# Layer 0 of a graph network: one-hots of the matmul lots compared on VectorE instead of turned on TensorE, with the helper steps of the next batch in other places

## What is computed

```
h = relu(layernorm(x))
for each head:
    feat = h @ W[head];  alpha_s = feat @ a1;  alpha_d = feat @ a2
    logit = leaky_relu(alpha_s[src] + alpha_d[dst], 0.2)
    e = exp(logit - segment_max(logit, src)[src])
    att = e / segment_sum(e, src)[src]
    out = relu(segment_sum(att * feat[dst], src))
x = x + concat(out)
```

## Time and profile before

| | us |
|---|---|
| median of 3 runs | 3007.26 (3004.64 to 3008.09) |
| span of the profiled execution | 3541.0 |
| PE busy | 2699.5 |
| DVE busy | 2161.8 |
| POOL busy | 1858.0 |
| ACT busy | 995.2 |

### The profile page before, as it was taken

The page is one execution under the profiler, slowest core; times in us unless marked ns, Lnnn a source line. Parts: engine busy times, 40 slices in busy tenths (PEclk is TensorE's granted clock), DMA queues, the critical chain, the costliest instruction groups (busy, mean ns, idle before and its releaser), DMA issues. The chain is left out here.

```text
span 3541.0 us, 46052 instructions
## 1 busy us (share of the span) xinstructions
PE 2699.5 (76%) x10647; PEld 1671.1 (47%) x10692; DVE 2161.8 (61%) x3783; ACT 995.2 (28%) x3078; POOL 1858.0 (52%) x1883
## 2 busy tenths in 40 slices
PE   6887377777777877777777787877778788788991
PEld 4554256666656656655656652323333333233440
DVE  9999966666666767666668743333333333334668
ACT  6733334444443444434444520000000000000220
POOL 0000255555555556555555446666666666664667
PEclk8998678898988899898898897888889999999995
DMA  5110366666666666666665856666666666565226
GB/s 184 47 40 31 111 180 185 186 189 185 180 182 188 180 191 189 183 192 176 177 189 191 288 152 174 176 180 178 178 176 178 173 173 175 171 174 157 67 66 251
DMA packets 243449, 588.25 MB, mean 166 GB/s; under 512 B 57744, under 2 KB 82832, under 8 KB 243400
## 3 DMA queue, kind: packets, MB, share of 16 engines
q0 software_dynamic: 133120, 443.52, 43.8%
q1 hardware_dynamic: 110280, 144.14, 12.4%
HBM read 533.43 MB, written 54.10 MB: 166 GB/s over the span
## 5 line engine op out<-in xcount | busy, mean ns | idle before, releaser
L506 POOL DMA_INDIRECT big<-feat_table,idx x880 | 841.3, 956 | 1020.8 <-ACT idx L531 407.5
L1133 POOL DMA_INDIRECT big<-h_table,idx x784 | 743.6, 948 | 460.6 <-issue 235.2
L801 PE MATMUL psA<-big,onehot 128*128 128x260 f32 x1760 | 504.0, 436 | 120.1 <-DVE big L683 95.4
L801 PE MATMUL psB<-big,onehot 128*128 128x260 f32 x1760 | 479.8, 420 | 18.6 <-DVE acc L693 13.1
L801 PEld LDWEIGHTS psA<-big,onehot 128*128 128x128 f32 x1760 | 365.4, 216 | 208.3 <-issue 115.2
L557 ACT ACTIVATE big<-big,late_weights 128x65 f32<-128x65 f32 x1760 | 434.4, 343 | 0.0
L801 PEld LDWEIGHTS psB<-big,onehot 128*128 128x128 f32 x1760 | 351.5, 209 | 84.9 <-DVE acc L693 22.2
L531 ACT CAST idx<-minorB 128x8 int32 (+1 forms) x101 | 20.4, 204 | 1142.6 <-DMA big<-h_table,idx 1142.6
L1565 DVE TENSOR_TENSOR acc<-acc,psCD 128x512 f32 x176 | 120.7, 686 | 320.1 <-remote 106.2
L1565 DVE TENSOR_TENSOR acc<-acc,psA 128x512 f32 x176 | 120.7, 686 | 273.6 <-remote 103.3
L1859 PE MATMUL psA<-big,onehot 128*128 x352 | 199.3, 650 | 58.9 <-issue 42.7
(11 more groups left out here) (447 smaller groups left out, 3960.8 us busy)
## 6 DMA issues: line engine op xcount, KB each, us to landing
nodes_all<-slot_nodes SPq DMA_DIRECT2D x56, 512.0 KB
big<-feat_table,idx POOLq DMA_INDIRECT x880
feat_table<-big SPq DMA_DIRECT2D x49, 264.0 KB, 2.1
x_table<-acc SPq DMA_DIRECT2D x49, 256.0 KB, 3.8
h_table<-big SPq DMA_DIRECT2D x49, 256.0 KB, 4.0
big<-h_table,idx POOLq DMA_INDIRECT x784
big<-h_table SPq DMA_DIRECT2D x49, 256.0 KB, 2.6
big<-x_table SPq DMA_DIRECT2D x49, 256.0 KB, 4.3
```

The source lines that it names most:

```text
L506: g.indirect_dma_start(ring[:, b.k, q * SB + u, :], None, feat_table, bass.IndirectOffsetOnAxis(ap=idx[:, 2 * b.k + q, u:u + 1], axis=0)). ...
L801: ins = pet.matmul(psum[:, 512 * hf:512 * hf + HALF_W], onehot[:, q, u % SB, :], ring[:, b.k, u, HALF_W * hf:HALF_W * (hf + 1)], start=(u ...
L1133: g.indirect_dma_start(big[:, place:place + D], None, h1_table, bass.IndirectOffsetOnAxis(ap=idx[:, r.c % CHUNK_CYCLE, b:b + 1], axis=0)). ...
```

## The change

The float32 one-hots are no longer turned by PE and cast by ACT. The sorted source nodes, turned once in the setup, are kept in a tile `nodeA` (bfloat16). In each slot DVE, behind `add_lot`, compares the one-hots of the same lot of `nxt`: 128 node numbers in PSUM against the nodes of two chunks, 256 elements on each partition. PE's lots wait for them one by one. `turn_logits` stands one lot sooner on PE, `sum_ends` too; `local_runs` stands in slot 3 of DVE in place of 4, `carry_runs` in 5 in place of 4, `find_tops` and `make_factors` in 6 in place of 5. The second look-up stands behind lot 7. `pad_keys`, `nodeA` and `maxd` share one tile `spare`.

```diff
+        spare = sb("spare", [P, PAD_SPAN + TILES * H], F32)
+        nodeA = spare[:, 0:COLS // 2].bitcast(BF16).rearrange("p (b r) -> p b r", b=SB)
-        onehot_ps = psC[:, 0:512].bitcast(BF16)
+        numbers0 = psC[:, 0:P]
@@ layer0_sync
+            sp.wait_ge(look_ps, 2 * (BATCHES + 1))
@@ layer0_scalar
-            def keep_onehot(b, q):
-                act.wait_ge(turned_ps, b(2, q + 1))
-                s.copy(onehot[:, q, :, :].rearrange("p b n -> p (b n)"), onehot_ps).then_inc(onehot_ready, 1)
                 s.copy(logit, logit_ps).then_inc(logit_kept, 1)
-                keep_onehot(b, 0)
...
                 keep_parts(b.ahead(1))
-                if this:
-                    act.wait_ge(lot_ps, this(LB, LB + RING_CREDIT))
-                keep_onehot(b, 1)
...
+            act.wait_ge(fieldsT, 2)
+            act.wait_ge(nodes_out, 1)
+            s.copy(nodeA.rearrange("p b r -> p (b r)"), psB[:, :]).then_inc(nodes_kept, 1)
             clear_rest()
@@ layer0_vector
-                wait_count(dve, turned_ps, b(2, q - 1))
+                wait_count(dve, look_ps, b(2, q - 1))
...
+            def make_onehot0(b, a):
+                q, u = a // LOTS, 2 * a % SB
+                dve.wait_ge(lot_ps, b(LB, a + 1 - LB + RING_CREDIT))
+                v.tensor_tensor(onehot[:, q, u:u + 2, :], numbers0.unsqueeze(1).broadcast_to([P, 2, P]),
+                                nodeA[:, u:u + 2, bass.ds(b(2, q), 1)].broadcast_to([P, 2, P]), ALU.is_equal).then_inc(onehot_ready, 1)
...
-                        if a == 4:
+                        if a == 3:
                             local_runs(nxt)
+                        if a == 5:
                             carry_runs(nxt)
-                        if a == 5:
                             make_onehotT(aft, 1)
+                        if a == 6:
                             find_tops(nxt)
                             make_factors(nxt)
...
                         add_lot(this, a, tiles[a % LOTS])
...
-                    if nxt and a == 1:
-                        make_onehotT(aft, 0)
+                    if nxt:
+                        make_onehot0(nxt, a)
+                        if a == 1:
+                            make_onehotT(aft, 0)
...
+            link(v.tensor_copy(numbers0, iota_row[:, :]))
@@ layer0_tensor
-            def turn_onehot(b, q):
-                wait_count(pe, onehot_ready, b(2, q))
-                for u in range(SB):
-                    ins = pet.transpose(onehot_ps[:, u * P:(u + 1) * P], onehotT[q][:, u * P:(u + 1) * P], ident_b)
-                ins.then_inc(turned_ps, 1)
...
-                if a % LOTS == 0:
-                    pe.wait_ge(onehot_ready, b(2, q + 1))
+                pe.wait_ge(onehot_ready, b(LB, a + 1))
...
-                    if a == 0:
-                        turn_onehot(nxt, 0)
+                    if a == 2:
+                        turn_logits(nxt)
                     if a == 3:
-                        turn_logits(nxt)
-                    if a == 4:
                         sum_ends(nxt)
-                        turn_onehot(nxt, 1)
                     if a == 5:
                         spread_carries(nxt)
                     if a == 6:
-                        for q in range(2):
-                            look_up(aft, q, tiles[q])
+                        look_up(aft, 0, tiles[0])
                         spread_factors(nxt)
                         turn_weights(nxt)
+                    if a == 7:
+                        look_up(aft, 1, tiles[1])
```

More of the change, by code:

```diff
@@ L139, in build @@
         iota_pad = sb("iota_pad", [P, PAD_COLS], F32)
-        pad_keys = sb("pad_keys", [P, PAD_SPAN], I32)
+        spare = sb("spare", [P, PAD_SPAN + TILES * H], F32)
+        pad_keys = spare[:, 0:PAD_SPAN].bitcast(I32)
+        nodeA = spare[:, 0:COLS // 2].bitcast(BF16).rearrange("p (b r) -> p b r", b=SB)
         ones = sb("ones", [P, H], F32)
@@ L151, in build @@
         alphas = sb("alphas", [P, TILES, 2 * H], F32)
-        maxd = sb("maxd", [P, TILES, H], F32)
+        maxd = spare[:, PAD_SPAN:].rearrange("p (t h) -> p t h", t=TILES)
         Wa = sb("Wa", [P, KD, 2 * H], F32)
@@ L333, in build @@
         rows_arrived = [sem(f"rows_arrived{n}") for n in range(2 * ARRIVAL_GROUPS)]
-        turned_ps = sem("turned_ps")
+        nodes_kept = sem("nodes_kept")
         onehot_ready = sem("onehot_ready")
@@ L721, in pass_batch @@
                             tiles = load_tiles(dve, tileA, this(2, 1))
-                    if nxt and a == 1:
-                        make_onehotT(aft, 0)
+                    if nxt:
+                        make_onehot0(nxt, a)
+                        if a == 1:
+                            make_onehotT(aft, 0)
             dve.wait_ge(acc_zeroed, 3)
             dve.sem_inc(lot_added, ADD_CREDIT)
+            link(v.tensor_copy(numbers0, iota_row[:, :]))
+            dve.wait_ge(nodes_kept, 1)
             link(v.memset(running[0:H, 1, CH:CH + 1], -BIG))
```

## The result

| | median of the runs, us | range, us |
|---|---|---|
| before | 3007.65 | 3004.64 to 3008.09 |
| after | 3177.98 | 3174.15 to 3179.82 |

The ratio is 1.0572, with a 95% interval of 1.0559 to 1.0585: slower by 170 us. The forecast was 3110 with 2960 to 3195 around it; the sign and the range held, and the median lies 68 us above the forecast.

A forecast was written before the change was run, and what follows sets the result against it. POOL's gathers were taken to bound both loops, at 20.05 us a pass in layer 0. The new pass was 17.8 + 2.6 + 1.5 = 21.9 us; 54 x 1.85 = 100, plus 2, gave about 3110 us, range 2960 to 3195.

The forecast's parts named there:

- clock falls behind the end sums: PE's lot 4 in layer 0's loop: slowdown after idling, left out of the sum and priced only as rival B.
- rival B: PE idles some 3 us before the end sums, clock falls, lot 4 late by 1.9 us: 103 on top, 3213 us; chance 0.14.
- DVE waits for lot 4: Layer 0's loop: lot 4 queues on PE behind the end sums, so DVE waits 1.48 us in each pass.
- DVE's work over the gathers' pace: Layer 0's loop: comparisons raise DVE's work from 17.8 to 20.4 us a pass, passing POOL's 20.05.
- What bounds the kernel: Both layers' loops run at POOL's gather pace without a profile, 20.05 us a pass in layer 0; nameless waits come from recording.
- Rival A: Gathers faster than 1.25 us without a profile, so DVE's 19.1 us chain binds today: 3160 us; chance 0.10.
- C: PE's stalls partly real, and the new order relieves DVE's waits in layer 0: faster, 2945 us; chance 0.20.
- D: Landing of the gathers sets the pass at about 21.9 us, comparisons fill DVE's waits: 3007 us; chance 0.10.
- The cost of a comparison: Each 256-element DVE comparison takes about 420 ns, adding 0.33 us a step, 2.6 us a pass (ends 2.2 and 4.9).
- DVE's slack: Layer 0's loop before: DVE's chain of 19.1 us a pass leaves 0.95 us under the gathers' pace.
- The waits at the old L635 and L652: DVE's waits for `sum_ends` (0.4 us a pass) and `spread_carries` (0.9) go in the new order.

The follow-up runs named there:

- filler: Changed kernel plus 12 float32 matmuls on PE just ahead of the end sums, product overwritten by lot 4: 3116.58 us, ratio 1.0378.
- end sums later: Changed kernel with the end sums back behind lot 4 on PE, all else as changed: 3035.55 us, ratio 1.0112.
- fewer gathers: Kernel before with 12 of 16 gathers issued in a pass from batch 2 on (results wrong): 2984.43 us, ratio 0.9937.
- the two and eight operations: Kernel before plus two or eight unused 256-element DVE operations a pass: 3012.74 us (ratio 1.0035) and 3086.2 us (ratio 1.0288).
- the order alone: Kernel before's one-hots (PE turns, ACT casts) with the change's slots for the other steps: 3025.45 us, ratio 1.0077.
- Comparisons alone: Changed kernel's one-hot comparisons with every step of the order back in its slot of before: 3067.6 us, ratio 1.0218.

## Why the prediction was right in sign and 68 us short

The 172 us (1.0572 x 3003) divide as follows, each part from two runs that differ in it (the filler itself costs some 5 us, which stand in the second part and are missing from the first):

| part | from | us | forecast |
|---|---|---|---|
| clock falls behind the end sums | after less filler | 58 | 0 (rival B: 103) |
| DVE waits for lot 4 | filler less end sums later | 80 | 1.48 x 54 = 80 |
| DVE's work over the gathers' pace | end sums later less before | 34 | 0.35 x 54 = 19 |

**What bounds the kernel.** Right. Both loops ran at the pace of their gathers (20.04 us a pass against 20.05), and the nameless waits were the recording's. In layer 0 the run with fewer gathers tests this; in layer 1 only the match of the times and POOL's row speak for it. Rival A, faster gathers and no slack, fell with the same two runs and with the two and eight operations. (A slip in the working: eight lots at 1.81 us are 14.5 us, not 14.1; nothing hangs on it.) C, which had PE's stalls partly real, fell with that, and so did the gain it promised. D fell too: the pass follows DVE's load.

**The cost of a comparison.** Right in what one takes, 416 ns for about 420. What it adds to DVE's busy time is a bit less than forecast: 1093.96 us with the end sums one lot later, less 976.27 before, is 117.7 over 432 comparisons, 0.27 us each and 2.2 us a pass. That is the low end of the range given, and 2.6 was taken.

**DVE's slack.** Mis-sized: 0.95 forecast, 0.4 measured (fewer gathers). The forecast counted two waits of DVE's chain and missed two of 0.33 us a pass. Here two errors nearly cancel: with the end sums later, DVE's busy time is 19.9 us a pass, not 20.4, and its pass is 20.64, since some 0.7 us of small gaps remain that the forecast put at nothing.

**The new wait of DVE for lot 4.** Right in place, mechanism and size: 1.48 us forecast, 1.47 with the clock kept up. PE waits at L778 in every pass, DVE behind it, and the wait is gone when the end sums stand behind the lot. The waits at the old L635 and L652 went as forecast. The pass without the clock's part would be 21.9 us by the forecast and is 22.1.

**The clock.** This is the step that failed, and most of the 68 us: it was put at nothing in the sum and measured 58. The forecast worked out PE's idle time before the end sums well (some 3 us; 2.96 in the pass shown) and had a slow lot after a wait in the earlier trace rows. It then gave rival B 0.14, because "the waits of the trace that were followed by a slow lot are as long or longer". An idle time equal to one that had been followed by a slow lot is an argument for the rival, not against it. Nor was it so for this lot: the earlier trace rows show only its own 0.15 us of idling, and the wait before it, one small matmul earlier, was 2.30 us, shorter than the 3 us forecast:

```profile
1060.48 0.61 PE L779 MATMUL psE<-look_space,heads 8*128 8x32 f32 x2 [2.30 <-DVE look_space L645]
```

The clock fell in 45 of the 54 passes. The rival's price was too high in turn: 1.45 us a pass (23.5 less 22.05), not 1.9, and 58 us by the timed runs, not 103. The Trainium skill (TensorE: Matmul & The Clock Gate, Part 1) has the array at 1.2 GHz after idling; these runs agree, with 3.66 us for the lot behind 2.96 us of idling. They also show that the length of that one wait does not settle it: 9 waits of 2.96 to 2.99 us left the clock up, and one of 1.73 us, in the order alone, was followed by a lot of 3.71.

**The parts do not add.** Comparisons alone cost 65 us and the order alone 23, 88 together; the change costs 172. The likely reason is that each uses the slack that the other would need. Without comparisons, PE idles half as long at the end sums, the clock holds, and DVE can afford its wait. With them, DVE reaches the local runs later, so PE idles about 3 us, and DVE has nothing left to pay with. The placement of the end sums costs 15 us beside the old one-hots (1.0077 less 1.0028) and 138 beside the new ones.

## What to carry to other kernels

A step that waits for another engine, put into an in-order queue ahead of work that the same engine is waiting for, makes both wait. Put it behind the piece of work that its producer needs next, even if its result comes later. If PE has idled as long as a change would now have it idle in each pass, or less, and a slow lot followed, price the slow lot in the forecast. Measure slack before it is spent: take away what sets the pace, or add two operations that nobody reads. And compare a recording's span with the timed runs before trusting any wait in it.

## What the runs showed of the hardware that was not expected

One recording of the same program was 541 us longer than another (3541.0 against 2999.7 us), 532 of it in the two loops (1432.8 and 1162.6 against 1096.8 and 967). There DVE had nameless waits of up to 4.8 us in layer 0 and 14.1 in layer 1, and the granted clock was 0.90 in place of 1.00; the second recording had neither.

PE idle for 3 us in a loop where it is otherwise busy was followed by a slow stretch at 1.2 GHz in 45 of 54 passes. Behind waits of about 1.5 us in every pass (the comparisons alone) it kept 2.4 GHz. In between it went either way: of waits of 1.7 to 2.3 us in two other runs, 12 were followed by a slow lot, and others as long as 1.99 us were not. Kept busy with products that nobody reads, PE kept 2.4 GHz too, and the kernel with more PE work was the faster one.
